# Where GpSimd makes the second half's k*v and the fifth sum, in a fused cross-attention and RWKV kernel

## The reference

```python
xn = _ln(x, ln1_w, ln1_b)
sx = _token_shift(xn, state[:, i1])                    # previous token minus this one
xxx = jnp.tanh((xn + sx * maa_x) @ maa_w1).reshape(b, l, 5, 1, EXTRA_MAA)
xxx = jnp.matmul(xxx, maa_w2).reshape(b, l, 5, E)
x5 = xn[:, :, None] + sx[:, :, None] * (maa_stack + xxx)          # five mixed inputs
w = jnp.exp(-jnp.exp(time_decay + jnp.tanh(x5[:, :, 1] @ decay_w1) @ decay_w2))
r, k, v = x5[:, :, 3] @ Wr.T, x5[:, :, 0] @ Wk.T, x5[:, :, 2] @ Wv.T
g = jax.nn.silu(x5[:, :, 4] @ Wg.T)
def step(s, rkvw):                                     # 32 heads of 8 channels, over 64 tokens
    a = k_t[:, :, :, None] * v_t[:, :, None, :]
    out = jnp.einsum('bhk,bhkd->bhd', r_t, u * a + s)
    return (a + w_t[:, :, :, None] * s, out)
...
x = x + att * g @ Wo.T                                 # att: outs, normalised per head
xn2 = _ln(x, ln2_w, ln2_b)
sx2 = _token_shift(xn2, state[:, i0])
x = x + sigmoid((xn2 + sx2 * ffn_maa_r) @ ffn_Wr.T) * (square(relu((xn2 + sx2 * ffn_maa_k) @ ffn_Wk.T)) @ ffn_Wv.T)
```

## Time and profile before

| | |
|---|---|
| median of 3 executions | 692.4 us (690.88 to 697.16) |
| profiled execution, its own time | 689.89 us |
| its span, first to last instruction | 688.0 us |
| TensorE, busy share of the span | 613.5 us (89%) |
| VectorE | 574.1 us (83%) |
| ScalarE | 390.5 us (57%) |
| GpSimd | 294.1 us (43%) |
| TensorE's clock, mean granted | 0.983 of full |
| a steady pass | 59.2 us (first sum at 388.56 and at 447.73) |

### The profile page before, as it was taken

One profiled execution on the slowest core, in us unless ns is written; L12 is line 12 of the kernel. 1 busy time (PEld: TensorE's weight loads), 2 busy tenths in 40 slices (PEclk: granted clock), 3 DMA queues, 4 the chain that ended last, 5 costly groups with the idle time before them and its releaser, 6 DMA issues.

```text
span 688.0 us, 9610 instructions
## 1 busy us (share of the span) xinstructions
PE 613.5 (89%) x2694; PEld 332.2 (48%) x2694; DVE 574.1 (83%) x902; ACT 390.5 (57%) x933; POOL 294.1 (43%) x210
## 2 busy tenths in 40 slices
PE   8999999979787859899899989989988998995896
PEld 5666666647232224354445435344543534443475
DVE  2999999973568898978997997899799789959944
ACT  3888888853443354567365455737546464353343
POOL 1111363002035293475639428464851946590020
PEclk9999999999999999999999999999999999998699
DMA  2343222201270841456267055526706540670020
GB/s 68 121 124 105 83 72 61 83 13 31 77 168 0 154 92 31 80 135 124 31 153 143 10 106 131 99 30 152 152 4 127 131 74 4 149 153 30 0 31 30
DMA packets 42444, 57.87 MB, mean 84 GB/s; under 512 B 4978, under 2 KB 25106, under 8 KB 42418
## 3 DMA queue, kind: packets, MB, share of 16 engines
q1 hardware_dynamic: 33008, 46.77, 29.6%
q0 software_dynamic: 9104, 10.77, 8.9%
q10 hardware_dynamic: 306, 0.02, 0.0%
HBM read 16.13 MB, written 7.86 MB: 35 GB/s over the span
## 4 chain that ended last, share of the span: by engine, by line
PE 29%; DVE 17%; issue 11%; POOL 7%; ACT 4%; DMA 1%; SPq 1%; DVEq 0%; POOLq 0%; ACTq 0%
PE ps_a L793 9%; DVE state L1459 8%; PE ps_c L878 6%; PE ps_c L793 3%; POOL x L683 2%; POOL state L656 2%; DVE vb L1464 2%; PE ps_att L858 2%; DVE x L1419 2%; PE ps_a L816 1%; PE ps_a L821 1%; DVE sx L1537 1%; DMA vb<-v 1%; PE ps_c L931 1%; POOL xn L646 1%
## 5 line engine op out<-in xcount | busy, mean ns | idle before, releaser
L683 POOL TENSOR_TENSOR x<-x,xn 128x1024 f32<-128x1024 f32 x35 | 86.2, 2471 | 151.0 <-DVE x L1419 151.0
L1459 DVE TENSOR_TENSOR_SCAN state<-ps_w,state 128x512 f32<-128x512 f32 x128 | 145.8, 1200 | 0.2
L793 PE MATMUL ps_a<-x,wsq 128*128 128x512 f32 x256 | 119.3, 610 | 10.1 <-POOL x L683 7.5
L656 POOL TENSOR_TENSOR state<-vb,k 128x2016 f32<-128x2016 f32 x23 | 105.3, 4577 | 27.0 <-DVE state L1446 10.4
L1464 DVE TENSOR_TENSOR vb<-state,r 128x2048 f32<-128x2048 f32 x32 | 86.1, 2692 | 1.7
L793 PEld LDWEIGHTS ps_a<-x,wsq 128*128 128x128 f32 x256 | 48.5, 195 | 68.9 <-issue 59.4
L1419 DVE SCALAR_TENSOR_TENSOR x<-ps_a,vec,sx 128x512 f32<-128x512 f32 x80 | 56.2, 745 | 27.7 <-PE ps_a L816 15.9
L310 ACT ACTIVATE probs<-ps_f,negmax 128x256 f32<-128x256 f32 x128 | 59.0, 473 | 1.9 <-DVE negmax L364 1.1
L816 PE MATMUL ps_a<-mix_t,w 64*128 64x512 f32 x128 | 47.6, 634 | 9.8 <-ACT mix_t L1161 7.1
L1117 ACT ACTIVATE zn<-wyz,rs 128x256 f32 (+1 forms) x60 | 31.1, 594 | 22.5 <-POOL rs L640 22.5
L374 DVE TENSOR_SCALAR probs<-probs,rowinv 128x256 f32<-128x256 f32 x128 | 41.8, 369 | 2.2
(11 more groups left out here) (213 smaller groups left out, 1259.3 us busy)
## 6 DMA issues: line engine op xcount, KB each, us to landing
vb<-v SPq DMA_DIRECT2D x120, 256.0 KB, 5.5
x<-in_x SPq DMA_DIRECT2D x32, 128.0 KB, 2.1
c<-in_ctx SPq DMA_DIRECT2D x32, 128.0 KB, 2.3
wyz<-in_x POOLq DMA_DIRECT2D x7, 512.0 KB, 5.9
out<-wyz SPq DMA_DIRECT2D x7, 512.0 KB, 7.4
out<-sx POOLq DMA_DIRECT2D x7, 512.0 KB, 6.4
vb<-v SPq DMA_DIRECT2D x16, 128.0 KB, 2.4
wsq<-in_wsq POOLq DMA_DIRECT2D x7, 256.0 KB, 3.2
```

The source lines that it names most:

```text
L656: nc.gpsimd.tensor_tensor(st[q][:, :, :, 1:L], src[:, :, :, 0:L - 1], wide(k[p][h][:, :])[:, :, :, 0:L - 1], ALU.mult).then_inc(kv_at(n, h ...
L683: nc.gpsimd.tensor_tensor(x5[j % 2][:, :, :], x5[j % 2][:, :, :], xn[:, :, 1:L1], ALU.add).then_inc(x5_ready, 1)
L793: mm = nc.tensor.matmul(bank[:, :], wsq[:, weight, c, P * o:P * o + P], src(c), start=(c == 0), stop=(c == EC - 1))
L1459: nc.vector.tensor_tensor_scan(row, w[h][:, :], row, 0.0, ALU.mult, ALU.add).then_inc(scanned, 1)
```

## The change

In `body`, GpSimd makes k*v of part (1,0) ahead of the first sum instead of behind it, and ahead of that waits until `c_gn` of chunk n-1 is complete on VectorE (a new helper, `hold_gated`). In `first_pass`, the fifth sum goes ahead of the next chunk's k*v (0,0). No instruction other than the wait is added or removed, and no other engine's order changes.

```diff
+            def hold_gated(n):
+                pool.wait_ge(ag_ready, n * 2 + 2)
+
             def hold(n):
                 pool.wait_ge(bonus_ready, n * 2 + 2)
...
@@ first_pass
                 z_add(n + 2)
                 add_x(n + 1, 2)
                 add_x(n + 1, 3)
+                add_x(n + 1, 4)
                 b_kv(n + 1, q, 0, 0)
-                add_x(n + 1, 4)
                 rstd(n + 2, ln1_var, ln1_rstd, ve1, rs1)
                 b_kv(n + 1, q, 0, 1)
...
@@ body
                 prev(n - 1, sx2_ready, xprev2, t["prev0"], xn2)
                 prev(n + 1, sx_ready, xprev, t["prev1"], xn)
+                hold_gated(n - 1)
+                b_kv(n, p, 1, 0)
                 add_x(n + 1, 0)
-                b_kv(n, p, 1, 0)
                 if z:
                     z_add(n + 2)
                 add_x(n + 1, 1)
```

## The result

The changed kernel takes 697.08 us (median of 20 executions, 694.93 to 702.61), the kernel before 693.14 (20, 689.89 to 697.88): ratio 1.0066, interval 1.0048 to 1.0084. It is 4 us slower, and the interval leaves 1 out. I had forecast 8.7 us faster.

What follows compares the result with a forecast made beforehand. Each pass was taken as a VectorE stretch, then a packed TensorE stretch. Gains of 6.9 (n = 1 to 5) + 2.0 (first pass) - 0.15 (n = 6) = 8.7 us gave 692.4 - 8.7 = 683.7 us; range 680 to 691.

Steps and rivals of the forecast that it cites:

- What bounds a pass: Steady pass: a VectorE stretch, then a packed TensorE stretch; VectorE time saved before 408.85 moves the second stretch's start.
- the 1.38 us of the forecast: Passes n = 1 to 5: gain taken per pass, from product (0,1) at 2.29 us; 6.9 us in all.
- the margins that I had worked out: Steady passes: 0.4 to 0.5 us at new x and decay; TensorE idle 2.8 us in all.
- something hidden ends last: Rival: new x, decay or GpSimd's rstd uses up its margin; a pass gives 0.7 to 0.9, total 687.1; chance 0.17.
- the slow rival: Steady passes: `a_mod` on VectorE is shut out by the new k*v; +13, 705 us; chance 0.04.
- The step that failed: Passes n = 1 to 5: product (0,1) comes during `z_add`'s issue and ends at 395.92 instead of 397.31, 1.39 us saved.
- The 0.8 us that I considered for the issue: Steady passes: if VectorE starved `z_add`'s issue of descriptors, the second sum would end 0.8 us later, near 398.9.
- The margin: Steady passes: product (0,1) comes at 393.63, 0.48 us after the first sum's end.
- the product meets the first sum instead: Rival: k*v starts over 0.48 us late, product waits for the 2.18 us sum; 690 to 695 us; chance 0.09.
- n = 6: Sixth pass, without `z_add`: the second sum starts at once and holds up the product; VectorE gains nothing, -0.15 us at most.
- The first pass: Fifth sum runs in idle time ahead of k*v (0,0); 2.0 us gain taken, between 1.3 and 2.6.
- the bounds: First pass: 1.3 us from the next chunk's earlier product (0,0); 2.6 if the clock holds and `c_gn` comes earlier.

Runs made afterwards that it cites:

- the two runs above: The change plus a VectorE memset of 128x256, or of 128x512, between scans and product: 696.63 and 694.95 us, one execution each (kernel before: 690.54).

## Why the prediction was wrong

**What bounds a pass** was right. When the product takes 2.29 us instead of 3.68, a pass takes 57.8 instead of 59.2, the 1.38 us of the forecast, and when it takes 5.4 the pass takes 60.8. No other wait took the gain away in the kernels in which the product is bare; the margins that I had worked out for the new x, the decay, the rstd and TensorE's idle time held. The rival in which something hidden ends last, 0.17, is refuted by the same runs, and so is the slow rival: `a_mod` is 0.745 us in the mean of 80, as before.

**The step that failed** is: the product "finds GpSimd issuing `z_add`, and runs its bare 2.29 us". I took from the earlier trace rows that the instruction behind an issue starts 0.83 us after it, and so that a product that comes earlier has the port. It came at 0.21 (0.21 to 0.50 in the five passes) and did not get it. The sum that stood ready behind the issue went first each time. In the kernel before the product had always been waiting when the chain began: it had asked during k*v, got the port at its end, and only then came the issue. The row of the issue beside the executing product looked like a proof that the two go together; it showed only the case in which VectorE was first. With the two in the other order no row of before could show the result, so this was an unknown cost, and I had put it at nothing where it should have been bounded by the remainder of the issue and a whole sum: 1.1 + 2.2 = 3.3 us, less the 1.4 won, so 1.9 a pass (measured: 1.6). Five passes of that are 9.5 us of loss against 2 won, which is 700, and my range ended at 691.

The 0.8 us that I considered for the issue in the sentences on the Trainium skill was the wrong price for the same place: not the sum is late but the product. The rule there speaks of descriptors that starve, and the issue got no longer: it took 1.27 to 1.34 us in the steady passes of every kernel.

**The margin.** I had 0.48 us between the first sum's end and the product. It was 0.15 in n = 3, since k*v starts 0.36 us after `c_gn` ends (390.72 against 388.95 + 1.41), not 0.1. In the loop (n = 1 to 4) k*v starts 0.24 to 0.36 us after it, in n = 5 and 6, which are written out, 0.09. In n = 5 the margin was 0.45, about as I had said, and the product still took 5.17 us: it was not the margin that failed. The rival "the product meets the first sum instead" took the point from which it decides for a danger. It is the opposite: with the product there before the first sum is over and the issue behind it, a pass is 57.9 us.

**n = 6** was right: without an issue the second sum goes first, and the product takes 3.84 us, 0.15 more than before.

**The first pass** was right in its mechanism; its size was 2.8 us (3.1 in the trace), taken at 2.0 within 1.3 to 2.6. I had named the clock as what decides between the bounds, and so it is, but they lie at 0.7 and 3.1. The two products are 4.34 and 3.26 us as worked out (4.3 and 3.4). The clock was granted in full from 252 to 264 us (before 0.86 from 250 to 262), TensorE's pause ahead of the turn fell from 3.40 to 1.25, and VectorE then no longer waits 1.0 us ahead of `c_gn`.

## What to carry to other kernels

When two engines take turns at a port, what decides is who asks first, and a move of 0.1 us can turn it round: list for each meeting who comes first, by how much, and what the winner has queued behind. If GpSimd issues a DMA near such a meeting, count a large piece of its ready work behind the issue as one block with it (the few small copies behind add_out did not shut the product out); keep it back with a wait for the event at which the other engine comes. Idle time on GpSimd right behind the block (4.25 us here) says that GpSimd can afford this wait; that the reader of the sum can too shows in the pass, 57.8 us with the wait and with the memset in its place.

## What the runs showed of the hardware that I had not expected

- An issue of a DMA on GpSimd with a ready 128x1024 sum behind it shut out a VectorE product with two SBUF inputs that came 0.2 to 0.9 us after the issue's start; the product took 4.75 to 5.5 us instead of 2.29 (5.3 to 5.6 with a small copy ahead of the sum). The same issue with a sum that became ready only after the product came: 2.29. A memset of 0.90 us in the issue's place with a ready sum behind: 2.29.
- Behind an issue GpSimd's records overlap by 0.5 us (2.70 for a sum of 2.18), over at least three instructions, and a product that had waited 0.8 us was not let in between two sums. Without an issue ahead, a product that had waited 1.4 us was let in between k*v and a sum that stood ready behind it (n = 6 of before), and one that had waited 0.16 us between a sum and an issue.
- Open: behind add_out's issue ready copies don't shut the product out, 0.6 to 0.9 us into the issue, though their records overlap by the same 0.5 us. The moment is excluded by the two runs above, and a copy ahead of a sum changed nothing. Whether it is the direction of the DMA, or that no larger work was ready behind the copies, wasn't tried. One reading fits every row here, and no run tests it: ready work starts under the issue, not behind it. Then a sum of 2.18 us has the port before the product comes, a chain that runs on half a microsecond early never lets it go, and the four copies, 0.19 us each, are as good as over when the product comes 0.6 us after the issue's start. How the port is handed over inside the chip is inferred from lengths and starts alone.
